# Attention outputs scaled once per group of heads instead of probabilities scaled once per step, in a decoder on one core

## What is computed

```python
scores = jnp.einsum('bhqd,bhkd->bhqk', q, k) / scale      # a0: times decay; a1: causal mask
attn = jax.nn.softmax(scores, axis=-1)
out = jnp.einsum('bhqk,bhkd->bhqd', attn, v)
x = _layernorm(x + out @ W_o, axis=-1)
```

## Time and profile before

| what | us |
|---|---|
| median of 3 runs (4370.3 to 4377.9) | 4376.41 |
| the profiled execution | 4397.46 |
| its span | 4395.7 |
| busy: TensorE, VectorE | 3439.4, 2820.9 |
| busy: ScalarE, GpSimd | 2073.9, 1385.9 |
| a0, a1, x1 (by the start of their first loads and the blocks behind) | 939, 1110, 857 |

### The profile page before, as it was taken

The page is one execution under the profiler, slowest core; times in us unless marked ns, Lnnn a source line. Parts: engine busy times, 40 slices in busy tenths (PEclk is TensorE's granted clock), DMA queues, the critical chain, the costliest instruction groups (busy, mean ns, idle before and its releaser), DMA issues. The chain is left out here.

```text
span 4395.7 us, 81705 instructions
## 1 busy us (share of the span) xinstructions
PE 3439.4 (78%) x25420; PEld 2507.5 (57%) x25421; DVE 2820.9 (64%) x7262; ACT 2073.9 (47%) x4994; POOL 1385.9 (32%) x1108
## 2 busy tenths in 40 slices
PE   5878788758689588888888879999998409999970
PEld 3555555537678356666556556777767306666650
DVE  5888888868867488888888846666666311121116
ACT  4777777753242165555555536555555101111110
POOL 1333333324300376666665702122222350000004
PEclk9999999988799799999899989999999559999995
DMA  2000000010010211111111110000000720010013
GB/s 68 6 7 7 7 7 7 1 34 19 25 74 1 66 44 35 30 44 37 35 40 31 33 41 7 11 6 6 6 1 1 242 80 27 29 31 29 29 35 105
DMA packets 101919, 147.71 MB, mean 34 GB/s; under 512 B 19904, under 2 KB 71552, under 8 KB 100800
## 3 DMA queue, kind: packets, MB, share of 16 engines
q1 hardware_dynamic: 95424, 126.58, 9.5%
q0 software_dynamic: 6144, 16.79, 1.2%
HBM read 61.52 MB, written 31.46 MB: 21 GB/s over the span
## 5 line engine op out<-in xcount | busy, mean ns | idle before, releaser
L1012 DVE TENSOR_SCALAR a_t<-a_t,a_inv 128x512 f32<-128x512 f32 (+3 forms) x768 | 719.1, 979 | 9.0
L695 PE MATMUL a_T<-ident,a_t 128*128 128x128 f32 x3328 | 535.3, 300 | 163.8 <-DVE a_t L1012 89.8
L854 ACT ACTIVATE a_t<-a_t,a_neg 128x512 f32<-128x512 f32 (+3 forms) x1024 | 642.5, 634 | 7.7 <-DVE a_neg L1040 7.3
L845 ACT ACTIVATE a_pT<-a_T 128x512 f32<-128x512 f32 (+3 forms) x1024 | 484.7, 514 | 328.1 <-PE a_T L695 324.6
L695 PEld LDWEIGHTS a_T<-ident,a_t 128*128 128x128 f32 x3328 | 402.7, 151 | 379.8 <-issue 217.0
L884 POOL TENSOR_TENSOR a_t<-a_t,a_inv 128x512 f32<-128x512 f32 x256 | 284.4, 1133 | 653.5 <-DVE a_inv L1008 653.5
L1035 DVE CUSTOM_DVE_ANT_0 a_t<-a_A,a_decay 128x512 f32<-128x512 f32 x512 | 322.7, 685 | 91.0 <-PE a_A L655 89.3
L884 POOL TENSOR_TENSOR x_t<-x_t,x_inv 128x576 f32<-128x576 f32 x128 | 158.1, 1257 | 696.3 <-DVE x_inv L1008 696.3
L2096 DVE COPY experts_y<-experts_Y 128x256 f32<-128x256 f32 x72 | 30.6, 425 | 513.9 <-PE experts_Y L2034 513.9
L909 POOL TENSOR_TENSOR a_rsin<-a_rawswapped,a_sin 128x512 f32<-128x512 f32 x128 | 170.1, 1329 | 583.5 <-DMA a_rawswapped<-a_raw 558.7
L1035 DVE CUSTOM_DVE_ANT_0 a_t<-a_A,a_table 128x384 f32<-128x384 f32 (+3 forms) x512 | 224.1, 485 | 128.5 <-PE a_A L667 125.6
(11 more groups left out here) (273 smaller groups left out, 7243.1 us busy)
## 6 DMA issues: line engine op xcount, KB each, us to landing
a_rawswapped<-a_raw SPq DMA_DIRECT2D x512, 64.0 KB, 2.0
ex_w<-in_f_w_dram SPq DMA_DIRECT2D x16, 1024.0 KB, 13.6
moe_sent<-route_zeros SPq DMA_DIRECT2D x1, 9216.0 KB, 29.5
experts_xg<-moe_sent SPq DMA_DIRECT2D x72, 128.0 KB, 2.0
moe_results<-experts_y SPq DMA_DIRECT2D x72, 128.0 KB, 1.7
a_xin<-x_all SPq DMA_DIRECT2D x16, 512.0 KB, 4.1
x_xin<-x_all SPq DMA_DIRECT2D x16, 512.0 KB, 2.9
x_all<-in_x_dram SPq DMA_DIRECT2D x1, 4096.0 KB, 14.9
```

Source lines behind the costliest of these rows:

```text
L695: mm = pe.transpose(bank[:, kt, :], t_of(u, j, kt * P, (kt + 1) * P), sh.ident[:])
L845: nc.scalar.activation(to, of, ACT.Copy).then_inc(t_empty, 1)
L854: nc.scalar.activation(t_of(u_e % U, j, 0, n), t_of(u_e % U, j, 0, n), ACT.Exp, bias=neg[:, slot, j:j + 1], scale=SCALE, accum_out=total[: ...
L1012: nc.vector.tensor_scalar(t_of(u_n % U, j, 0, m), t_of(u_n % U, j, 0, m), inv[:, u_n % 4, j:j + 1], None, ALU.mult).then_inc(normed, 1)
```

## The change

- The probabilities stay unnormalised. GpSimd has no work in a0 and x1, and VectorE's L1012 is gone in all three.
- The reciprocals of unit u are kept (`inv`, now U slots) and *spilled*: SyncE writes 128 x 4 numbers of 4 bytes to rows of a DRAM tensor `inv_rows` (L507 after), one DMA a unit. After SPAN units (8 in a0, 4 in a1 and x1) SyncE waits for these, *spreads* the rows over the partitions of the heads in `inv_rep` (L522 after; 8 DMAs of 16 x 512 numbers in a0, 2 of 64 x 2 x 512 in a1 and x1), and waits for them to land.
- VectorE multiplies O by `inv_rep` into `oT` (L1036 after), in place of ScalarE's copy, once in SPAN units (one product in a0, two in a1 and x1), ahead of the score reductions of the step. It waits for the values of the group's last unit and for the spread.
- In a0 VectorE copies the fourth transposed head (L1030 after), with a semaphore `t_copied` of its own, in place of ScalarE.
- The transposes wait for `exped`, the exponentials, alone.
- SyncE's program is now written by steps like the others: in a step the next batch's load, the spread, the spill, then the swaps of a1.
- `fold_butterflies` loads its matrices in two groups (3 and 4 stages), not three (2, 2 and 3).

```diff
--- before.py
+++ after.py
...
@@ -236,8 +236,8 @@
     Y_AT = [(LAG_V, 1), (LAG_V, 3), (LAG_V + 1, 1), (LAG_V + 1, 3)] if x1 else \
         [(LAG_V + i, 0 if a0 else 1) for i in range(QT)]
     LN_STEP = Y_AT[-1][0] + 1
-    POOL_HEADS = () if a1 else (2, 3)
-    DVE_HEADS = 4 - len(POOL_HEADS)
+    SPAN = 8 if a0 else 4
+    COPIES = 8 if a0 else 2
     V_CUT = 256
     IN = FH if a1 else 512
...
@@ -346,7 +346,9 @@
         mx1 = sb("mx1", [P, 4, 4])
         neg = sb("neg", [P, 4, 4])
         total = sb("total", [P, 4, 4])
-        inv = sb("inv", [P, 4, 4])
+        inv = sb("inv", [P, U, 4])
+        inv_rep = sb("invrep", [P, 1 if a0 else 2, S])
+        inv_rows = nc.dram_tensor(f"{kind}_inv_rows", (2, SPAN, S), F32).ap()
         stats = sb("stats", [P, QT, 6])
         mv = sb("mv", [P, QT, 2])
         scratch = sb("scratch", [P, 3, QT])
...
@@ -495,25 +499,56 @@
                     sp.dma_start(raw_swapped[32 * k:32 * k + 32, n % 2, :],
                                  raw[32 * (k ^ 1):32 * (k ^ 1) + 32, n % 4, :]).then_inc(swapped[n % 2], 16)
...
-                        if n == 3:
-                            sp.wait_ge(xt_done, b * DT + DT)
-                            sp.dma_start(xin[:], sh.x_all[:, bass.ds(b * QT + QT, QT), :]).then_inc(xin_in, 16)
-                for n in range(4 * G):
-                    swap_halves(B - 1, n)
-                return
-            with sp.Fori(1, B) as b:
-
-                sp.wait_ge(xt_done, b * DT)
-                sp.dma_start(xin[:], sh.x_all[:, bass.ds(b * QT, QT), :]).then_inc(xin_in, 16)
-                if x1:
-
-                    sp.wait_ge(v_done, b * N_V)
-                    sp.dma_start(ctxT[:], w["ctxT"][bass.ds(b, 1)].rearrange("a (t p) n -> p (a t) n", p=P))\
+            def spill(b, u):
+
+                g, qt = divmod(u % U, QT)
+                rows = inv_rows[g // 2 % 2, g % 2::2] if a0 else inv_rows[g % 2]
+                wait_apart(sp, (weights, 16 * len(loads)), (inverted, b * U + (u + 1)))
+                sp.dma_start(rows[:, qt * P:(qt + 1) * P].rearrange("j p -> p j"), inv[:, u % U, :], allow_slow_non_contiguous=True)\
+                  .then_inc(spilled[u % U // SPAN % 2], 16)
+
+            def spread_rows(b, k):
+
+                per = U // SPAN
+                p = k % per % 2
+                wait_apart(sp, (weights, 16 * len(loads)),
+                           (spilled[p], b * (per // 2 * SPAN * 16) + (k // 2 + 1) * SPAN * 16))
+                for c in range(COPIES):
+                    if a0:
+                        to, of = inv_rep[16 * c:16 * c + 16, 0, :], inv_rows[p, c:c + 1, :].to_broadcast([16, S])
+                    else:
+                        to = inv_rep[64 * c:64 * c + 64]
+                        of = inv_rows[p, c::2, :].unsqueeze(0).to_broadcast([64, 2, S])
+                    sp.dma_start(to, of).then_inc(spread, 16)
+                wait_apart(sp, (weights, 16 * len(loads)), (spread, b * (per * COPIES * 16) + (k + 1) * COPIES * 16))
+
+            def step(b, s, prev, own, nxt):
+                if s == 0 and nxt:
+                    sp.wait_ge(xt_done, b * DT + DT)
+                    sp.dma_start(xin[:], sh.x_all[:, bass.ds(b * QT + QT, QT), :]).then_inc(xin_in, 16)
+                if x1 and s == LAG_V and nxt:
+                    sp.wait_ge(v_done, b * N_V + N_V)
+                    sp.dma_start(ctxT[:], w["ctxT"][bass.ds(b + 1, 1)].rearrange("a (t p) n -> p (a t) n", p=P))\
                       .then_inc(ctx_in, 16)
+                u_n = s - LAG_N
+                if s < U and u_n % SPAN == 0 and (own if u_n > 0 else prev):
+                    spread_rows(b, u_n // SPAN - 1)
+                if s < U and (own if u_n >= 0 else prev):
+                    spill(b, u_n)
+                for _, work in tasks(s, prev, own, nxt):
+                    if a1 and work[0] == "item":
+                        swap_halves(b + (work in NEXT and s >= U - QT), 4 * work[1] + work[2])
+
+            def begin():
+                for work in START:
+                    if a1 and work[0] == "item":
+                        swap_halves(0, work[2])
+
+            def body(seg, turn, b, prev, own, nxt):
+                for s in range(U if own else LN_STEP):
+                    step(b, s, prev, own, nxt)
+
+            batches(sp, begin, body)
 
         @block.tensor
...
@@ -681,14 +716,9 @@
             def transpose_head(b, ug, u, j):
 
                 job = ug * T_UNIT + j
-                by_dve, by_pool = min(j + 1, DVE_HEADS), min(j + 1, 4) - DVE_HEADS
-                waits = [(normed, ug * DVE_HEADS + by_dve)] + \
-                    ([(normed_pool, ug * len(POOL_HEADS) + by_pool)] if by_pool > 0 else []) + [(t_empty, job + 1)]
-                if j < 4:
-                    for sem, value in waits:
-                        pe.wait_ge(sem, value)
-                else:
-                    wait_apart(pe, (ready, N_READY), *waits)
+                free = [(t_empty, job + 1)] if not a0 else \
+                    [(t_copied, ug + 1)] if j == 1 else [(t_empty, ug * 3 + (2, 0, 3, 4)[j])]
+                wait_apart(pe, (ready, N_READY), (exped, ug * 4 + min(j + 1, 4)), *free)
                 bank = T[(u * T_UNIT + j) % 2]
                 if j < 4:
                     for kt in range(keys(u) // P):
...
@@ -739,7 +769,11 @@
                     score_head(seg, turn, b, s, 4)
                 if do_v:
 
-                    pe.wait_ge(t_empty, (b * U + u_v + 1) * T_UNIT + 2)
+                    if a0:
+                        pe.wait_ge(t_empty, (b * U + u_v + 1) * 3 + 2)
+                        pe.wait_ge(t_copied, b * U + u_v + 2)
+                    else:
+                        pe.wait_ge(t_empty, (b * U + u_v + 1) * T_UNIT + 2)
                     g, qt = divmod(u_v % U, QT)
                     if u_v >= 0 and qt == 0 and (not a0 or g == 0):
                         pe.wait_ge(*(seg.emptied(turn, ("v", 0, N_V - 1)) if a0 else (v_done, b * N_V + (g + 1) * N_V // G)))
...
@@ -835,7 +868,7 @@
 
                     act.wait_ge(pv, b * U + (u_t + 1))
                 for j in range(5):
-                    if do_t and j < T_UNIT:
+                    if do_t and j < (3 if a0 else T_UNIT):
                         u = u_t % U
                         act.wait_ge(t_full, (b * U + u_t) * T_UNIT + (j + 1 + T_CREDIT))
                         bank = T[(u * T_UNIT + j) % 2]
...
@@ -854,14 +887,6 @@
                         nc.scalar.activation(t_of(u_e % U, j, 0, n), t_of(u_e % U, j, 0, n), ACT.Exp,
                                              bias=neg[:, slot, j:j + 1], scale=SCALE,
                                              accum_out=total[:, slot, j:j + 1]).then_inc(exped, 1)
-                if do_v:
-                    g, qt = divmod(u_v % U, QT)
-                    if qt == QT - 1 and (not a0 or g % 2 == 1):
-
-                        act.wait_ge(pv, b * U + (u_v + 1 + 2))
-                        for o in ([g // 2] if a0 else [0, 1]):
-                            nc.scalar.activation(oT[:, o if a0 else 2 * g + o, :], O[o][:],
-                                                 ACT.Copy).then_inc(o_empty, 1)
 
             def begin():
                 for work in START:
...
@@ -875,25 +900,6 @@
 
         @block.gpsimd
         def _(pool):
-            def step(b, s, prev, own, nxt):
-                u_n = s - LAG_N
-                if s < U and (own if u_n >= 0 else prev):
-
-                    pool.wait_ge(inverted, b * U + (u_n + 1))
-                    for j in POOL_HEADS:
-                        nc.gpsimd.tensor_tensor(t_of(u_n % U, j, 0, NK), t_of(u_n % U, j, 0, NK),
-                                                inv[:, u_n % 4, j:j + 1].to_broadcast([P, NK]),
...
@@ -1000,22 +1009,32 @@
                 found = tasks(s, prev, own, nxt)
                 u_n = s - LAG_N
                 do_n = s < U and (own if u_n >= 0 else prev)
+                u_v = s - LAG_V
+                do_v = s < U and (own if u_v >= 0 else prev)
                 slot, qt, n = s % 4, s % QT, keys(s)
                 at = S - P - qt * P if (a0 or a1) else 0
                 for j in range(5):
                     if do_n and j == 0:
                         dve.wait_ge(exped, (b * U + u_n + 1) * 4)
-                        nc.vector.reciprocal(inv[:, u_n % 4, :], total[:, u_n % 4, :]).then_inc(inverted, 1)
-                        dve.wait_ge(inverted, b * U + (u_n + 1))
-                    if do_n and j < DVE_HEADS:
-                        m = NK if x1 else keys(u_n % U)
-                        nc.vector.tensor_scalar(t_of(u_n % U, j, 0, m), t_of(u_n % U, j, 0, m),
-                                                inv[:, u_n % 4, j:j + 1], None, ALU.mult).then_inc(normed, 1)
+                        nc.vector.reciprocal(inv[:, u_n % U, :], total[:, u_n % 4, :]).then_inc(inverted, 1)
                     if own and prev and LN_STEP <= s <= LN_STEP + 1:
                         advance(norm[0], 2)
```

(17 more changed lines are left out.)

23 lines of the change are left out of this document (7 added, 16 removed).

## The result

The changed kernel takes 4747.43 us (median of 4 runs, 4712.93 to 4752.44), the kernel before, measured again beside it, 4373.35 us (4366.06 to 4377.9). The ratio is **1.084, 95% interval 1.079 to 1.089**: 8.4% slower, where I had forecast 5% faster. Its profiled execution spans 4745.4 us.

The account below looks back on a forecast made before the run. It took a0 and a1 as held by VectorE's normalisation work and waits for low parts and probabilities. Terms -92 - 124 - 9 + 2 + 4 = -219 us from 4397.46 profiled, less 21 for the median, gave 4157 us; range 4070 to 4275.

Parts of the forecast that it names:

- the one on SP's queue: New spills and spreads in every attention step: a spill lands in 3 us, the rest is covered by other work, 0.
- Rival 3: Slower: 4 B spills fill the DMA queues and pace the attention; about 4600 us at a drain of 8 us; chance 0.05.
- its formula: With a drain of D us per spill, a batch takes 16 D in a0 and about 16 D + 15 in a1.
- a0: forecast -92: First attention: batch falls from 108.5 to 97 us, middle of 89.9 and 104.4, ScalarE pacing a bare step at 4.74 us.
- a1: forecast -124: Causal attention: batch falls from 133.5 to a middle of 118 us, with 5 us of rotation wait a batch inside.
- My upper end: In a1, only the 8.8 us wait for probabilities goes, leaving 124.7 us a batch.
- Rival 2: All waits go, so the kernel is faster than forecast; 111 us a batch for a1; chance 0.10.
- rival 1: Clock and rotation keep the gain small, half-clock stretches lengthening transposes in ScalarE's chain: -106 us, 4270 us; chance 0.23.
- x1: forecast -9: Attention over input and context: already full, some ScalarE copies and VectorE waits go; -9 us, bounds -24 and +4.
- folding: Matrix loads in two groups, not three: first matmuls wait for 1.5 MB, not 1 MB; +2 us, between 0 and +4.
- The ends: After each attention's last exponential, spill and spread replace 1 to 2.5 us of normalisation: +4 us in all.
- The signs that I had named: Signs of error: spill landing after 7 us, product waiting in each group, rotation wait over 5 us a batch, clock staying 0.90.

Follow-up runs that it names:

- the ladder: Kernel before with transfers timed ahead of its first attention, nothing else running: one adjacent 4 B spill 8.6 and 12.2 us, sixteen 109.5 us.
- half-sized: Changed kernel with spills of two heads' factors of four, 256 pieces of 4 B instead of 512: 4379.42 us.
- unwatched spills: Changed kernel spilling constant data every second unit, adjacent 4 B pieces, no landing waits before a stage's end, no spreads: 4277.07 us; pieces 64 B apart: 4171.64 us.
- the ladder by distance: Kernel before with spills of 4 B pieces at distances of 4 to 512 B timed ahead of its first attention: one spill 15.5 down to 1.9 us.
- the turned version: Changed kernel with reciprocals block-transposed on VectorE and spilled once a span as 128 pieces of 128 B: 4196.52 us, ratio 0.955 to the kernel before.

## Why the prediction was wrong

**The step that failed** is the one on SP's queue: a spill of 512 pieces of 4 B lands in 3 us and drains in 0.6 to 1.6 us, "The rest lies beside other work: **0**". It landed in 13 us, and 8.6 to 15.5 us on a quiet chip. I bounded it from 256 pieces of 256 B and 1 KB pieces of one large transfer, by their number; neither row has several pieces in 64 B, and the bound of 3.6 us was none. Instead of 0 the spills cost 435 + 113 + 30 = 578 us in the three stages. (The whole spans differ by 4745.4 - 4182.5 = 563 us; the run without spills has the long end behind x1.)

**Rival 3** named the mechanism with its place, and gave it a chance of 0.05. It took the drain as the pace of the batch. It comes out near that in a0: a batch of (942.41 - 162.29) / 5 = 156 us is D = 9.8 by its formula, against 6.8 to 9.6 us a spill in the ladder. In a1 the formula gives another D: 140.8 us a batch is D = 7.9. And the half-sized and the unwatched spills, which by their drains should not fill a queue, cost 10 us a batch of a0 each. So the loss seems to be delay as well as a full queue. No row showed pieces of 4 B, and that gap deserved more than a rival with 0.05. The size of a piece alone does not make the cost: pieces of 4 B that lie 64 B apart cost 2.5 us for one spill, while adjacent ones cost 15.5. The stride between the heads, 2 or 4 KB in the kernel, is not what decides here either: in the ladder by distance it is 64 KB in every step, as the program writes it, and the time goes from 15.5 to 1.9 us with the distance along the queries.

**The other terms**, from the run without spills against the kernel before, whose stages by these bounds are 938.9, 507.1, 1128.4, 822.5 and 982.4 us:

- a0: forecast -92, measured -112. The batch came out at 99.7 us for my 97, and an undisturbed step of the changed kernel at 4.78 us (first score product to the next, 454.05 to 458.83) for my 4.74. What was off was the kernel before. I divided the 651.7 us of seven loads by six; the first of these intervals is short, since batch 0 has no batch before it. The last five loads alone give

```profile
227.99 457.62 SPq L511 DMA_DIRECT2D a_xin<-x_all  x5
```

  (457.62 - 0.49) / 4 = 114.3 us a batch, not 108.5. VectorE's share in a0 was to be 64% and is 68%.
- a1: forecast -124, measured -66.5; the batch went from 134.3 to 126.5 us, not from 133.5 to 118. My upper end was 124.7, "only the wait for probabilities goes", and that is nearly what happened. The middle of 118 us, and with it the -124 in the sum, had a lower end of 111 us under it, an estimate of mine that no run shows. In one batch of the turned version (1755.97 to 1882.64, 126.7 us) the clock is 0.95 and TensorE busy 110.8 us. Rival 2, over half of which the range reaches, had the same 111 us for a1; no run here took less than 4171.64 us in all. The waits there, between 1504 and 2135 us, 5.0 batches:

```profile
PE a_A L709 <- POOL a_khl L932: 26.4, 5, 6.2
PEld a_A L660 <- DVE a_mx L1066: 25.5, 5, 5.1
```

  The rotation costs 5.3 us a batch, as I had counted (5), once each. What I had not: the value projections wait 5 us a batch for the bank that the last score reductions free. The middle between two far ends was the fault; the upper one had a named wait behind it, the lower one only that estimate. GpSimd hardly got faster without VectorE's normalisation: it is busy 680.0 us in a1 without spills, against 687.8 before. The half-clock stretches of rival 1 are in the trace of the kernel before: from 598 to 600 us the clock is 0.50, and the eight transposes at 598.18 take 1.97 us, against 1.14 for the eight at 563.75, where it is 1.00.
- x1: forecast -9 with a lower bound of -24, measured -33.7. The batch went from 99.1 to 93.8 us. "Full already" took a busy TensorE for one that can't get shorter; its busy time itself fell from 740.2 to 728.5 us.
- folding, with all between a0 and a1: forecast +2, measured +2.7. The ends (+4) lie inside the stages and can't be read apart; what follows x1 changed by -3.2.

Together -213 us for my -219, once the spills are taken away. That the sum is so near is luck: a0 and x1 came out 20 and 25 us better than forecast and a1 58 us worse. **The signs that I had named** for being wrong appeared: a spill landing after 7 us, VectorE's wait for the spread (121.0 us in 22 waits in all), the rotation over 5 us a batch (90.6 us in 11 waits), and a clock that did not rise (0.79 in a0, 0.89 in a1).
